# Row work of an attention layer moved between slots and engines; the softmax weights' low parts divided two to one

## What is computed

```python
h = ssm_kernel(x)                      # complex exponentials, 32 x 128 x 1024
h = concat([h, txt], axis=1)           # 32 batches of S = 205 rows, D = 1024
h = h + attn(layernorm(h))             # 32 heads, 8 key/value heads, head dim 32, causal
h = h + ffn(layernorm(h))              # W_base, plus masked low-rank updates through an inverse real FFT
```

## Time and profile before

| | us |
|---|---|
| median of 3 runs (2894.68 to 2900.92) | 2897.89 |
| the profiled execution | 2894.3 |
| its span, first to last instruction | 2891.9 |
| TensorE busy in the span | 2655.3 |
| VectorE busy | 1941.2 |
| ScalarE busy | 1230.0 |
| GpSimd busy | 1144.9 |
| mean granted TensorE clock, share of full speed | 0.975 |

### The profile page before, as it was taken

How to read it: one execution, slowest core, us unless ns; L and a number is a source line. 1 busy time by engine, 2 the same in 40 slices (tenths; PEclk the granted TensorE clock), 3 DMA queues, 4 the chain that set the end, 5 groups by cost and what they waited for, 6 DMA issues and landing times. The chain is left out here.

```text
span 2891.9 us, 70053 instructions
## 1 busy us (share of the span) xinstructions
PE 2655.3 (92%) x27456; PEld 1919.6 (66%) x27456; DVE 1941.2 (67%) x5569; ACT 1230.0 (43%) x2570; POOL 1144.9 (40%) x1810
## 2 busy tenths in 40 slices
PE   1948999999999999999999976999999999999999
PEld 1838888888888888888888952444444444444444
DVE  8966888888888888888888674644444444444443
ACT  4343676766767676766667572201000010101010
POOL 2751565656656565666656570101010101010100
PEclk9979999999999999999999976999999999999999
DMA  7756556465555555565555454454545455545553
GB/s 242 194 122 100 98 92 105 85 109 93 96 94 96 103 93 104 84 107 92 101 92 86 73 124 170 113 139 116 133 122 136 119 134 121 133 123 131 125 129 77
DMA packets 509031, 332.99 MB, mean 115 GB/s; under 512 B 421145, under 2 KB 464409, under 8 KB 508225
## 3 DMA queue, kind: packets, MB, share of 16 engines
q1 hardware_dynamic: 486192, 264.68, 46.3%
q10 hardware_dynamic: 22512, 63.84, 7.1%
HBM read 116.49 MB, written 80.61 MB: 68 GB/s over the span
## 5 line engine op out<-in xcount | busy, mean ns | idle before, releaser
L1044 PE MATMUL psJ<-xth,qh 128*128 128x205 f16 x2048 | 517.3, 253 | 51.6 <-DMA xtl<-xfl 47.6
L704 POOL TENSOR_TENSOR pl<-arena,ph 128x410 f16<-128x410 f32 (+1 forms) x512 | 501.0, 998 | 94.7 <-ACT ph L790 94.7
L1046 PE MATMUL psJ<-xth,ql 128*128 128x205 f16 x2048 | 516.3, 252 | 0.0
L1045 PE MATMUL psJ<-xtl,qh 128*128 128x205 f16 x2048 | 515.8, 252 | 0.0
L699 POOL TENSOR_SCALAR_AFFINE_SELECT arena<-arena 128x256 f32<-128x256 f32 (+1 forms) x768 | 331.7, 438 | 438.3 <-ACT arena L783 419.3
L1261 POOL TENSOR_TENSOR arena<-stage,arena 128x1024 f32<-128x1024 f32 x52 | 122.1, 2349 | 936.2 <-DVE stage L1304 936.2
L1275 ACT CAST xh<-arena 128x1024 f16<-128x1024 f32 x52 | 54.3, 1045 | 995.1 <-DVE arena L1313 995.1
L783 ACT ACTIVATE arena<-psT,escale 128x410 f32<-128x410 f32 (+1 forms) x768 | 399.6, 565 | 95.5 <-PE psT L984 57.5
L790 ACT CAST ph<-arena 128x410 f16<-128x410 f32 (+1 forms) x768 | 334.8, 500 | 14.9 <-POOL arena L699 14.7
L1304 DVE SCALAR_TENSOR_TENSOR stage<-ps5O,osc,h_in 128x512 f32<-128x512 f32 x104 | 77.9, 750 | 388.4 <-PE ps5O L1401 388.4
L885 DVE TENSOR_REDUCE mx<-psS 77x2 f32<-77x410 f32 x512 | 296.5, 579 | 60.7 <-PE psS L1031 57.0
(11 more groups left out here) (231 smaller groups left out, 6106.2 us busy)
## 6 DMA issues: line engine op xcount, KB each, us to landing
a_in<-acat SPq DMA_DIRECT2D x52, 512.0 KB, 3.8
h_in<-hcat SPq DMA_DIRECT2D x52, 512.0 KB, 4.6
qst<-qsh SPq DMA_DIRECT2D x128, 205.0 KB, 4.7
out<-stage SPq DMA_DIRECT2D x51, 512.0 KB, 3.1
hcat<-ob SPq DMA_DIRECT2D x64, 256.0 KB, 4.4
xin<-hcat ACTq DMA_DIRECT2D x32, 512.0 KB
acat<-arena ACTq DMA_DIRECT2D x64, 256.0 KB
qst<-qsl SPq DMA_DIRECT2D x64, 205.0 KB, 5.7
```

The lines of the kernel that those rows point to most:

```text
L704: pool.tensor_tensor(view(pl, g % 2, k), view(p32, g % 2, k), view(ph, g % 2, k), ALU.subtract).then_inc(lo_pool, 1)
L1044: pe.matmul(ps[:, 0:S], wh[:, k, c], xth[:, par, k, 0:S], start=k == 0, stop=False)
L1045: pe.matmul(ps[:, 0:S], wh[:, k, c], xtl[:, par, k, 0:S], start=False, stop=False)
L1046: m = pe.matmul(ps[:, 0:S], wl[:, k, c], xth[:, par, k, 0:S], start=False, stop=k == KC - 1)
```

## The change

In `ssm` the peaks are taken two chunks earlier and stored one chunk earlier. In `attention`:

- The k and v units stand in slots 1 to 4 in place of 0 to 3. Where a q unit is followed by another unit, VectorE splits it within the slot, ahead of the layer norm and the normalisation.
- The rows of batch b+3 are made in step b, the step in which they are transposed, no longer a step earlier. ScalarE scales and centres in one operation and casts in a second, pieces 0, 1, 2 and 3 in slots 1, 2, 3 and 3, behind the first unit's cast. The low parts are made by GpSimd (`low_rows`) in slots 2, 3, 4 and 4. The reciprocal root moves from behind slot 3 to behind slot 4 on GpSimd, with one link more; its buffers are doubled.
- Of the three `pl` parts VectorE makes 0 and 1, GpSimd part 2.
- ScalarE copies one value tile in slot 1 and one in slot 2. Loads of rows and stores of output are issued by SyncE.
- SyncE's order becomes: restack of the second halves, second shift rows, store, transposes of the image rows, restack of the first halves, transposes of v, transposes of the text rows, first shift rows, store, load. In the steps before 0 the row transposes stand before those of v. Each of the small loads for the tail is issued in a step of its own from step 1; the large one in step 29.
- At the start, VectorE refines the first batch's reciprocal root itself, and the splitting of the weights is interleaved with the first batch's pieces; GpSimd clears only the third parts of `ph` and `pl`.

The diff, cut to its core:

```diff
@@ -168,10 +168,11 @@
             for dst, src, arrived in ahead:
                 sp.dma_start(dst, src).then_inc(arrived, 16)
             for ch in range(NCH):
-                if ch == NCH - 1:
+                if ch == NCH - 2:
                     sp.wait_ge(peaks_ok, 1)
                     sp.dma_start(acat[0, 0:2 * P].rearrange("(p t) -> p t", t=2), peaks[:]).then_inc(peaks_out, 16)
+                if ch == NCH - 1:
                     sp.wait_ge(peaks_out, 16)
                     sp.dma_start(all_peaks, acat[0:1, 0:2 * P].broadcast_to([P, 2 * P])).then_inc(peaks_in, 16)
...
-                if ch >= NCH - 12:
-                    weight_peak(ch - (NCH - 12))
-            dve.wait_ge(piece_ok, 12)
-            dve.tensor_reduce(peaks[:, 0:1], pieces[:, 0:8], AX.X, ALU.max)
-            dve.tensor_reduce(peaks[:, 1:2], pieces[:, 8:12], AX.X, ALU.max).then_inc(peaks_ok, 1)
+                if NCH - 14 <= ch < NCH - 2:
+                    weight_peak(ch - (NCH - 14))
+                if ch == NCH - 3:
+                    dve.wait_ge(piece_ok, 12)
+                    dve.tensor_reduce(peaks[:, 0:1], pieces[:, 0:8], AX.X, ALU.max)
+                    dve.tensor_reduce(peaks[:, 1:2], pieces[:, 8:12], AX.X, ALU.max).then_inc(peaks_ok, 1)
...
-        EXTRA = {0: ("v", 0), 1: ("v", 1), 2: ("k", 0), 3: ("k", 1)}
+        EXTRA = {1: ("v", 0), 2: ("v", 1), 3: ("k", 0), 4: ("k", 1)}
+        HIGH, LOW, LINK = {1: (0,), 2: (1,), 3: (2, 3)}, {2: (0,), 3: (1,), 4: (2, 3)}, {1: 0, 2: 1, 3: 2}
+        FIRST_HIGH, FIRST_LOW = {2: (0,), 3: (1,), 4: (2, 3)}, {3: (0,), 4: (1,), 5: (2, 3)}
...
-                if b == B - 2:
-                    for q in v_in:
-                        sp.wait_ge(q, 32 * B)
-                    for dst, src, arrived in ahead:
-                        sp.dma_start(dst, src).then_inc(arrived, 16)
-                if has["turn"]:
+                if has["last"]:
+                    store(b - 1, 1)
+                if has["turn"] and b >= 0:
 
                     wait(sp, pj_filled, base)
                     turn(0, nxt, b + 3)
-                    turn(1, nxt, b + 3)
                 if has["qkv"]:
 
                     wait(sp, pj_lo, base + at(rows, "k", 0) + 1)
@@ -614,16 +615,50 @@
                     restack(K_PARTS, kst[par][:, 0:4], slice(0, 1), k_in[0])
                     wait(sp, pj_lo, base + at(rows, "q", 3) + 1)
                     restack(Q_PARTS, qst[par][:, 0], HALVES[0], q_in[0])
+                if has["turn"] and b < 0:
+                    wait(sp, pj_filled, base)
+                    turn(0, nxt, b + 3)
+                    turn(1, nxt, b + 3)
+                if has["qkv"]:
+                    wait(sp, pj_lo, base + at(rows, "v", 1) + 1)
                     wait(sp, v_ok, 2 * (b + 2))
                     if b == -2:
                         sp.wait_ge(values_ok, 1)
                     for c in range(2):
                         for k in range(2):
                             sp.dma_start_transpose(out=vt[:, k, :, c * P:(c + 1) * P], in_=vst[k][:, c, :]).then_inc(v_in[c], 16)
+                if has["turn"] and b >= 0:
+                    turn(1, nxt, b + 3)
                 if has["max"]:
 
                     wait(sp, pj_lo, base + at(rows, "m", 0) + 1)
                     shift_rows(0, nxt)
+                if has["att"]:
+                    store(b, 0)
+                if has["load"]:
+                    sp.wait_ge(x_lo, 4 * (b + 4))
+                    load(b + 5, 1 - par)
+                if 1 <= b < len(ahead):
+                    dst, src, arrived = ahead[b]
+                    sp.dma_start(dst, src).then_inc(arrived, 16)
+                if b == B - 3:
+                    for q in v_in:
+                        sp.wait_ge(q, 32 * B)
+                    dst, src, arrived = ahead[0]
+                    sp.dma_start(dst, src).then_inc(arrived, 16)
...
                 r, cols = ((P, slice(0, P)), (TROWS, slice(P, P + TROWS)))[t]
+                sp.wait_ge(x_hi, 4 * n + 2 * t + 2)
+                sp.dma_start_transpose(out=xth[:, to, :, cols], in_=xfh[0:r, t, :]).then_inc(xt_in[t], 16)
                 sp.wait_ge(x_lo, 4 * n + 2 * t + 2)
-                sp.dma_start_transpose(out=xth[:, to, :, cols], in_=xfh[0:r, t, :]).then_inc(xt_in[t], 16)
                 sp.dma_start_transpose(out=xtl[:, to, :, cols], in_=xfl[0:r, t, :]).then_inc(xt_in[t], 16)
 
+            load(0, 0)
+            sp.wait_ge(x_in[0], 32)
+            load(1, 1)
...
                 pool.wait_ge(dve_ln, 9 * (b + 5))
-                rsqrt_rounds(links, pool, rs)
-                pool.tensor_scalar(nmean[:], mv[:, :, 0], -1.0, None, ALU.mult).then_inc(ln_done, 1)
+                rsqrt_rounds(links, pool, rs[:, b % 2])
+                links(pool.tensor_scalar(nmean[:, b % 2], mv[:, :, 0], -1.0, None, ALU.mult))
+                pool.tensor_tensor(nmean[:, b % 2], nmean[:, b % 2], rs[:, b % 2, 3], ALU.mult).then_inc(ln_done, 1)
+            def low_rows(m, n):
+                t, h = divmod(n, 2)
+                c, r = slice(h * D // 2, (h + 1) * D // 2), T[t]
+                pool.wait_ge(x_hi, 4 * m + n + 1)
+                pool.tensor_tensor(xfl[0:r, t, c], xin[0:r, m % 2, t, c], xfh[0:r, t, c], ALU.subtract).then_inc(x_lo, 1)
 
             links = Chain(pool, pool_ln)
 
             def step(b, par, has):
                 if not has["att"]:
-                    if has["ln"]:
+                    if has["ln"] and b > -4:
                         scale_rows(b)
+                    if has["turn"] and b > -3:
+                        for piece in range(4):
+                            low_rows(b + 3, piece)
                     if b == -4:
-                        pool.memset(ph[:], 0.0)
-                        pool.memset(pl[:], 0.0)
+                        pool.memset(ph[:, :, 2, :], 0.0)
+                        pool.memset(pl[:, :, 2, :], 0.0)
                     if b == -3:
                         pool.wait_ge(w_lo, 2 * KC)
                         pool.memset(p32[:, :, 2, :], 0.0).then_inc(late_ok, 1)
@@ -699,47 +748,39 @@
                         pool.affine_select(out=v, in_=v, compare_op=ALU.is_ge, fill=0.0, base=0,
                                            pattern=[[0, v.shape[1]], [1, w]],
                                            channel_multiplier=-1).then_inc(masked, 1)
-                    for k in (1, 2):
-                        pool.wait_ge(hi_done, 24 * b + 3 * g + k + 1)
-                        pool.tensor_tensor(view(pl, g % 2, k), view(p32, g % 2, k), view(ph, g % 2, k),
-                                           ALU.subtract).then_inc(lo_pool, 1)
-                    if g == 3 and has["ln"]:
+                    pool.wait_ge(hi_done, 24 * b + 3 * g + 3)
+                    pool.tensor_tensor(view(pl, g % 2, 2), view(p32, g % 2, 2), view(ph, g % 2, 2),
+                                       ALU.subtract).then_inc(lo_pool, 1)
+                    if has["turn"]:
+                        for piece in LOW.get(g, ()):
+                            low_rows(b + 3, piece)
+                    if g == 4 and has["ln"]:
                         scale_rows(b)
...
                 wait(act, av_done, 8 * (n - 1))
-                for k, dst in enumerate((vh, vl)):
-                    v = vt[:, k].rearrange("p t (g d) -> p t g d", d=HD)
-                    act.copy(dst[n % 2][:, :, :, 0:HD], v).then_inc(v_ok, 1)
+                v = vt[:, k].rearrange("p t (g d) -> p t g d", d=HD)
+                act.copy((vh, vl)[k][n % 2][:, :, :, 0:HD], v).then_inc(v_ok, 1)
...
-                    if g == 3 and has["load"]:
-                        act.wait_ge(x_lo, 4 * (b + 4))
-                        load(b + 5, 1 - par)
-                    if g == 2 and has["last"]:
-                        store(b - 1, 1)
-                    if g == 2 and has["max"]:
-                        values(b + 1)
-                    if g == 6 and has["att"]:
-                        store(b, 0)
                     if has["att"]:
                         for k in range(3):
                             act.wait_ge(st_filled, 24 * b + 3 * g + k + 1)
 
-                            if k:
-                                wait(act, lo_pool, 16 * b + 2 * (g - 2) + k)
+                            if k == 2:
+                                wait(act, lo_pool, 8 * b + g - 1)
                             else:
-                                wait(act, lo_done, 8 * b + g - 1)
+                                wait(act, lo_done, 16 * b + 2 * (g - 2) + k + 1)
...
+                    if g in (1, 2) and has["max"]:
+                        values(b + 1, g - 1)
+                    pieces = (HIGH if b >= 0 else FIRST_HIGH).get(g, ()) if has["turn"] and b > -3 else ()
+                    if not rows[g]:
+                        for piece in pieces:
+                            high_part(b + 3, piece)
+                    for i, (kind, m) in enumerate(rows[g]):
...
```

(42 more changed lines are left out.)

59 lines of the change are left out of this document (33 added, 26 removed).

## The result

| | before | after |
|---|---|---|
| median | 2897.38 (4 runs, 2894.68 to 2900.92) | 2847.12 (4 runs, 2845.32 to 2848.06) |
| profiled execution, its span | 2891.9 | 2844.7 |
| mean granted TensorE clock | 0.975 | 0.974 |

All in microseconds. The ratio is 0.9825 with a 95% interval of 0.9808 to 0.9842: the changed kernel is 50 us faster. The forecast was 2835 in a range of 2784 to 2884. Its direction and range held and its central value was 12 us too fast.

The account below looks back on a forecast made before the run. TensorE, busy 92%, was taken as the bound, with 3.7 us of stalls a step. Gains of 9 + 48 + 2 + 4 = 63 off 2891.9 gave 2829, adjusted to a median of 2835; range 2784 to 2884.

Parts of the forecast that it names:

- The steady step: Repeating steps: 44.8 us against 46.48, 1.7 gained in each of 28 steps, 48 us in all.
- Stalls of slots 0, 2, 5, 6 and 7: TensorE's waits in a steady step, 3.7 us together, expected to lose their old causes.
- the chain as written: Links delay slot 5's masks, then casts, subtractions and slot 6's maxima, ready at 3.65 for 2.03; 1.7 us charged.
- rival A: Steady steps: GpSimd is in time or its lateness absorbed, step 43.1, 48 us more gained, 2787; chance 0.18.
- The edges: VectorE's tight slack from one more subtraction per slot, charged 0.3 us a step, bounds 0 and 1.5.
- rival B: VectorE becomes the bound, short slots grow 0.2 to 0.4, step 46, 2869; chance 0.22 together with another rival.
- SyncE's queue: Six more transfers a step; shift rows land about 18, next step starts at 21: slack 3, cost nothing.
- Rival C: SyncE's queue delays shift rows and the next step's first scores; about 3000, or 2919 at half; chance 0.11.
- The start: Sequence before the repeating steps: net 9 us gained, bounds 1 and 13.
- The gain term: Start: first projection 12.5 us earlier, from earlier peaks, VectorE's reciprocal root and a sooner last transpose.
- The term given back: Start: 7.5 us lost to second-batch transposes (2.7), late shift rows (4.4) and VectorE's weight splits (0.5).
- Steps 28 and 29, the end: 2 us gained in steps 28 and 29 together, 4 from the last step's wait for shift rows.

Follow-up runs that it names:

- e1: Changed kernel with GpSimd's reciprocal-root links cut into three rounds of four, behind slots 5, 6 and 7, instead of all behind slot 4: 2798.2 us.
- e3: Changed kernel with VectorE making one low part of the softmax weights and GpSimd two, as the kernel before shared them: 2842.7 us.
- e2: Changed kernel with all the links one slot earlier, behind slot 3 instead of slot 4: 2802.4 us.
- e7: Changed kernel with e1's spread links and, in the steps before 0, shift rows and load issued ahead of the value transposes: 2787.9 us.
- e12: e8 with the first two row transposes also issued ahead of the restacks in the start: 2784.7 us.
- e8: e7 with GpSimd making the second and third batch's row low parts ahead of the next batch's links in the start: 2788.1 us.

## Why the prediction was right, and where it was not

**The steady step: right, by its own terms.** 44.8 was forecast and 44.76 measured; the loop gave 48.8 us for 48. Stalls of slots 0, 2, 5, 6 and 7 went, as said. GpSimd reaches slot 5's first mask at +4.30 (forecast +4.4), its pieces are 1.15 (1.21), and slot 6 is 1.76 longer (1.7; the chain as written gives 3.65 less 2.03, 1.6). e1 shows that the links' place is the cause, and with it rival A: its 2787, plus the 13 us by which the start was mis-sized, is 2800, and e1 took 2798. The edges, charged at 0.3, are not waits of VectorE: 24 of the 28 steps take 44.62 or 44.63, and the mean is 0.14 above that by four odd steps (46.51, 45.89, 44.79 and 45.09), the first of which begins at half clock.

**The shares.** I expected VectorE's doubled subtractions to have a slack of 0.1 to 0.5, and rival B to decide if it failed. It did not fail: with the links spread all slots are clean while VectorE makes two parts. The sum put the second subtraction into the chain behind the late masks (5.7 to 6.4), and e3 shows that it was there: taking it out gives back 0.5, as much as GpSimd's second part adds.

**SyncE's queue.** Nothing was paid, as costed, but the slack was half of the 3 us stated: the last shift row of the step shown is issued at 1048.72 and lands at 1051.97, 3.25 later and not 1.9, and the next step begins at 1053.60, so 1.6 is left.

```profile
1039.24 6.17 SPq L631 DMA_TRANSPOSE vt<-stage  x4
1045.45 1.27 SPq L670 DMA_TRANSPOSE xth<-xfh  x1
1046.77 1.27 SPq L672 DMA_TRANSPOSE xtl<-xfl  x1
...
1048.72 0.59 SPq L665 DMA_DIRECT2D qst<-ml  x1
```

Value transposes 6.17 (6.1), row transposes 1.3 each (1.4). Rival C did not come; but once the links are spread and the step is 1.75 shorter, more than that slack, it shows its face: in three to six of 28 steps of e1, e2, e7 and e12 slot 7 is 0.5 to 1.5 longer. One in e1, the first scores of the step that follows:

```profile
379.08 0.35 PE L1049 MATMUL psT<-qst,kst 98*128 98x410 f16 x1 [1.31 <-DMA qst<-ml]
```

**The start: wrong, by 13 us.** Forecast 9 gained, measured 4.4 lost. The gain term held: first projection 13.8 earlier for 12.5. But its parts as written add up to 11 to 12, and the size came out by luck: the last transpose is issued 8.1 earlier (207.18; 8 forecast) and then lands in 2.9 where it took 8.7, so 5.8 came from the landing and not 2 to 3. The table load that was to leave the way takes 1.28 in both kernels (at 288.68 and 291.81), so no run shows it as a gain.

The term given back was mis-sized. Forecast were 2.7 (second batch), 4.4 (shift rows), 0.5 (weight splits), and 3 us gained where ScalarE had held the second unit. Measured, as distances between starts less the usual 0.09: 3.1 for the second batch, 6.9 for the shift rows, 4.4 for units that wait for VectorE (0.8, 2.1 and 1.5), where before had 3.1; and two that were not in the sum, 3.0 for maxima behind statistics whose load stands behind value transposes, and 1.2 for a key's low part. Of such waits over 0.35 us from the first projection to step 0 there are 19.1 where before had 3.5, 15.6 more. The rest of the 18.3 is about what half the clock takes: TensorE's busy time by the missing share of the clock is 1.5 us from 246 to 250 and 1.6 from 259 to 265.

So no single step failed alone. In order of size: the 3 us to be won at the second unit did not come, since it now waits for VectorE, whose split at 218.75 stands behind statistics and the first guess (3.8 worse than forecast); the half clock after waits was not in the sum (3.1); moving the loads to SyncE's queue was costed at nothing (3.0); the shift rows were 2.5 later than put. The sum for the queue looked at the repeating steps, where eight slots of TensorE's work cover it, and not at the short steps before 0, where rows loaded behind four value transposes are wanted 4 us after the issue (249.43, and the statistics could begin at 253.5). The 2.7 came out at 3.1, but the cause given for it was wrong: e8 made the pieces earlier and nothing moved. Issuing the transposes earlier moved their landing by 0.55 only (e12), so the cause stays open.

**Steps 28 and 29, the end.** Forecast 2 and 4, measured 3.4 and 2.8: the wait of 4.09 is gone, step 31 begins without one, but a wait of 1.2 for shift rows now opens the second half of step 30. Behind that 3.4 us are given back, most of it in the tail, which the change does not touch: the two waits for the transfer of `in_fourier` are 10.47 and 9.13 for 9.12 and 8.24, and the matmuls behind them run at a granted clock of 0.50 (1734 to 1739) where before had 0.95 at the same place (1782 to 1785). Why, no run shows.
